# PSUM banks, one staged load, the weight splits and GpSimd's side jobs moved in the attention loops of an AdaLN block with experts

## The reference, cut to what matters

```
x: [4, 512, 256]                      # four batches of 512 tokens
mod = silu(c) @ wmod                  # per batch: shift, scale, gate of attention and of the FFN
h = layernorm(x) * (1 + ca) + sa
q, k, v = split(h @ Wqkv.T + bqkv)    # 16 heads of 16
scores = q k^T * 0.25, causal
attn = softmax(scores); x = x + ga * ((attn v) @ Wout.T + bout)
h = layernorm(x) * (1 + cb) + sb
top expert of 8 per token, its sigmoid scales the row
x = x + gb * (shared FFN(h) + FFN of the chosen expert)
```

## Time and profile before

| | |
|---|---|
| median of 3 runs | 470.62 us (469.96 to 471.55) |
| the profiled execution's own time | 467.88 us |
| its span, first to last instruction | 466.1 us |
| busy: PE, DVE, ACT, POOL | 86%, 67%, 49%, 45% |
| chain that ended last, by engine | PE 57%, DVE 16%, ACT 6%, POOL 6%, DMA 5% |
| mean granted TensorE clock | 0.969 |

### The profile page before, as it was taken

One profiled execution on the slowest core, in us unless ns is written; L12 is line 12 of the kernel. 1 busy time (PEld: TensorE's weight loads), 2 busy tenths in 40 slices (PEclk: granted clock), 3 DMA queues, 4 the chain that ended last, 5 costly groups with the idle time before them and its releaser, 6 DMA issues.

```text
span 466.1 us, 8603 instructions
## 1 busy us (share of the span) xinstructions
PE 401.6 (86%) x3009; PEld 226.4 (49%) x3009; DVE 313.4 (67%) x635; ACT 228.0 (49%) x408; POOL 211.4 (45%) x251
## 2 busy tenths in 40 slices
PE   3789984889879879878988878999998999999991
PEld 3244532334544446433544345565655666666660
DVE  7678594359888878998887853789844444444441
ACT  2445663577574757736777545345222323232320
POOL 2395952543227934368252862110510646464332
PEclk9999998699999999997999979999999999999997
DMA  8456489268942588945446201995531454434210
GB/s 269 159 131 143 164 237 227 91 184 212 257 112 90 175 190 261 288 133 169 128 137 213 62 1 46 344 358 202 148 123 46 73 96 72 89 65 87 27 20 0
DMA packets 46192, 67.96 MB, mean 146 GB/s; under 512 B 5380, under 2 KB 33668, under 8 KB 46152
## 3 DMA queue, kind: packets, MB, share of 16 engines
q1 hardware_dynamic: 31064, 36.74, 27.8%
q10 hardware_dynamic: 9936, 22.55, 14.8%
q0 software_dynamic: 5152, 8.14, 8.9%
HBM read 43.14 MB, written 25.18 MB: 147 GB/s over the span
## 4 chain that ended last, share of the span: by engine, by line
PE 57%; DVE 16%; ACT 6%; POOL 6%; DMA 5%; issue 5%; SPq 3%; ACTq 1%; DVEq 0%; POOLq 0%
PE bank L1504 35%; PE bank L1660 5%; PE bank L1644 4%; DVE mx L1137 3%; PE bank L1615 3%; DMA stage<-in_down 2%; PE bank L1885 2%; DMA qk_d<-W 2%; ACT W L887 2%; PE bank L1592 1%; SPq L532 1%; DVE x_sb L1182 1%; DVE rowg L1238 1%; POOL W L740 1%; POOL W L759 1%
## 5 line engine op out<-in xcount | busy, mean ns | idle before, releaser
L887 ACT ACTIVATE W<-bank 128x512 f32<-128x512 f32 (+1 forms) x176 | 93.8, 562 | 63.5 <-PE bank L1644 42.4
L1137 DVE TENSOR_REDUCE mx<-bank 128x1 f32<-128x384 f32 (+3 forms) x176 | 105.2, 633 | 26.2 <-PE bank L1617 22.5
L1504 PE MATMUL bank<-W 128*128 128x256 f16 (+2 forms) x756 | 104.7, 291 | 4.5 <-DVE x_sb L1182 1.8
L1504 PEld LDWEIGHTS bank<-W 128*128 128x128 f16 x756 | 73.0, 99 | 37.8 <-issue 8.2
L759 POOL TENSOR_SCALAR_AFFINE_SELECT W<-W 128x512 f32<-128x512 f32 x64 | 48.7, 764 | 86.9 <-ACT W L887 86.8
L1644 PE MATMUL bank<-W 128*128 128x512 f16 (+3 forms) x256 | 64.1, 308 | 20.1 <-ACT W L887 18.8
L1504 PE MATMUL bank<-W,h2T 128*128 x276 | 67.3, 380 | 0.8 <-issue 0.8
L830 POOL DMA_INDIRECT out<-h2T,sidx x23 | 36.3, 1578 | 64.1 <-DVE h2T L1474 63.8
L1615 PE MATMUL bank<-W 126*128 126x128 f16 (+3 forms) x208 | 53.6, 309 | 5.2 <-DVE mx L1137 4.7
L1660 PE MATMUL bank<-W 128*32 128x128 f32 (+3 forms) x512 | 49.6, 462 | 4.5 <-POOL W L759 4.4
L1644 PEld LDWEIGHTS bank<-W 128*128 128x128 f16 x256 | 21.5, 98 | 58.5 <-ACT W L887 36.7
(11 more groups left out here) (173 smaller groups left out, 557.3 us busy)
## 6 DMA issues: line engine op xcount, KB each, us to landing
w_d<-rowg ACTq DMA_DIRECT2D x18, 512.0 KB, 3.8
W<-w_d SPq DMA_DIRECT2D x18, 512.0 KB, 8.0
stage<-in_gup ACTq DMA_DIRECT2D x14, 512.0 KB
qk_d<-W SPq DMA_DIRECT2D x48, 128.0 KB
W<-qk_d SPq DMA_DIRECT2D x32, 192.0 KB, 5.5
stage<-in_down ACTq DMA_DIRECT2D x7, 512.0 KB
x_sb<-in_x SPq DMA_DIRECT2D x4, 512.0 KB, 8.9
h_d<-gbb SPq DMA_DIRECT2D x4, 512.0 KB, 4.6
```

The costliest lines, as they stand in the source:

```text
L887: a.activation(PT[j][:, i:i + m, :], t_bank(N)[:, 0:m * w].rearrange("p (i n) -> p i n", i=m), ACT.Exp).then_inc(s_exp, 1)
L1137: v.tensor_reduce(mx_v[:, b % 2, hp0 // 4, par, i:i + m, t], s_bank(N)[:, 0:m * w].rearrange("p (i n) -> p i n", i=m), AX.X, ALU.max).then ...
L1504: i = t_.matmul(outp, l, r, start=(n == 0), stop=(n == len(prods) - 1), **kw)
```

## The change

- The first pass goes round two banks (S0, S1) in the loops, the transposed pass round three (T0, T1, T2) all the way. The transposed unit 2 waits for the maximum of first-pass unit 32, which had T2 last. The waits follow the banks.
- SP issues the third staged load right behind `stacks(1, 0)`, ahead of `qk_out(1, 1)`, `stacks(1, 1)` and `mod_rows(0)`.
- SPLITS: eight weight units in b = 0 (n = 6, 12, 18, 23, 28, 33, 38, 43) where there were six, six in b = 1 at other steps, six in b = 2 (3, 10, 17, 24, 31, 38) where there were eight.
- POOL does its side jobs two steps later in the loops, save `rstd` and `bias_x`.

```diff
@@ SPLITS @@
-          0: {6: 0, 12: 1, 18: 2, 25: 3, 32: 4, 39: 5},
-          1: {2: 6, 9: 7, 16: 8, 23: 9, 30: 10, 37: 11},
-          2: {1: 12, 6: 13, 11: 14, 16: 15, 21: 16, 26: 17, 31: 18, 36: 19},
+          0: {6: 0, 12: 1, 18: 2, 23: 3, 28: 4, 33: 5, 38: 6, 43: 7},
+          1: {5: 8, 12: 9, 19: 10, 26: 11, 33: 12, 40: 13},
+          2: {3: 14, 10: 15, 17: 16, 24: 17, 31: 18, 38: 19},
...
+def gpsimd_jobs(b, n):
+
+    if b < 0:
+        return side_jobs(b, n)
+    prompt = ("stats1", "stats2", "bias")
+    return ([j for j in side_jobs(b, n - 2) if j[0] not in prompt]
+            + [j for j in side_jobs(b, n) if j[0] in prompt])
...
-        SB = [S0, S1, T2]
+        SB = [S0, S1]
...
-            return [S0, S1, T2, T0, T1, OTb][N % 6] if N < LAG else SB[N % 3]
+            return [S0, S1, T2, T0, T1, OTb][N % 6] if N < LAG else SB[N % 2]
...
-            return [T0, T1][N % 2] if N < BU * B - LAG else [T0, T1, T2][N % 3]
+            return [T0, T1, T2][N % 3]
...
             stacks(1, 0)
+            stage_load(2)
             qk_out(1, 1)
             stacks(1, 1)
             sp.wait_ge(s_md, 16)
             mod_rows(0)
-            stage_load(2)
...
-                    for job, c, k in side_jobs(b, n):
+                    for job, c, k in gpsimd_jobs(b, n):
...
-                if t_bank(N) is T2:
-                    pe.wait_ge(s_mx, BU * B)
+                if N == 2:
+                    pe.wait_ge(s_mx, LAG)
```

## The result

The changed kernel takes **468.4 us** (median of 20 runs, 464.0 to 472.74) against 470.24 (20 runs beside them); the ratio is 0.9939, 95% interval 0.9914 to 0.9964. The ratio leaves out the slow runs, those over 1.5% above the fastest of their kernel, so it says 2.9 us where the medians of all runs differ by 1.8. Against the 9.4 us that were forecast, the sign is right, the size is a third at most, and the forecast's own range of 456 to 467 us is missed by 1.4; the wide one, 453.0 to 470.0, holds it. The profiled execution took 466.85 us, span 465.1, granted clock 0.980 (before 0.969).

The account below looks back on a forecast made before the run. PE and DVE take turns at bounding the loops, with a stall in b = 0. Gains of 2.3 + 1.5 + 3.6 + 2.0 + 0 = 9.4 us off 470.62 give 461.2 us; forecast range 456 to 467, wide range 453 to 470.

Parts of the forecast that it names:

- Banks, taken as 0: Loops: fewer waits of transposed units for exps and more of first-pass units for maxima were taken to cancel; 0 us.
- the bounds, 18.6 us lost and 21.1 won: Banks in the loops: most that first-pass waits for maxima could lose, and most that waits for exps could return.
- The rival in which the first pass becomes the bound: Loops: PE waits for maxima and DVE lacks units; 9.2 us slower, 479.8 us, if all 18.6 are lost; chance 0.10.
- point of decision, 9.4 us lost: Banks: with half of the 18.6 us uncovered the time is 470.6, no change; above it the kernel is slower.
- Staged load, 2.3 us: Middle of b = 0: load issued earlier, ACT's wait goes, unit 22 starts at 83.4 us after the maxima's round trip.
- The first rival: Stall in b = 0: the maxima's trip ends when it did, only splits and masks are won; 465.0 us, chance 0.16.
- the sign set for it: Mark in b = 0: unit 22 starting at 85 us or later would show that the stall only changed its name.
- the second rival: Stall in b = 0: maxima share DMA engines with ACT's transfers, taking the load's 2.3 us; 463.5 us, chance 0.04.
- Clock behind the stall, 1.5 us: b = 0 behind the stall: PE stands about half as long, so the lower clock level may not fall or last less.
- Splits 3.6 and POOL 2.0 us: Splits: DVE time and half the lower-clock work in b = 2; POOL: about half of PE's 4.4 us mask waits.
- The mark "b = 2 shorter by 3 us": Sign for the splits: b = 2 shorter by 3 us or more; if as long as before, they did not set it.
- The rest: "no part of it to be given back": Behind the loops: unchanged work starts when they end, so none of the forecast 9.4 us was expected to be lost there.

Follow-up runs that it names:

- e3: The moved weight splits alone, on the kernel before; 471.46 us, ratio 0.9976.
- e4: The changed kernel with the banks of before (three for the first pass, two for the transposed pass); 465.85 us, ratio 0.9895 against the kernel before.
- e10: e4 with the staged load placed behind the writes of batch 1's second half, ahead of stacks, modulation rows and maxima; 462.95 us, ratio 0.9797.
- e12: The changed kernel with the third staged load put back behind the modulation rows; 471.01 us, ratio 1.0 against the kernel before.
- e15: e10 with PE's first-pass unit behind the values of each step instead of ahead of them; 464.43 us, ratio 0.9871 against the kernel before.
- e17: e10 with the new banks and PE's first-pass unit last in each step, behind values and side jobs; 462.79 us, ratio 0.9846.
- e7: e4 with the maxima of batch 0's second half sent out and in right behind the moved staged load; 472.18 us, ratio 0.9988.

## Why the prediction was right and wrong

**Banks, taken as 0: the step that failed.** The prediction said that where DVE is behind (residual, statistics, first norm) it "sets the pace with two banks as with three, and PE's wait moves without growing". It grew: 22 us more of first-pass waits, and 3.3, 2.1, 7.7, 3.9 and 6.7 us of time in five pairs, never a gain in this order of PE. I had looked at PE's wait and DVE's pace only; PE works in order, so the projections and transposed units queued behind the waiting unit waited too, and DVE then lacked units (with the banks alone, e1, 26.2 us of waits for PE, before 22.5; of the changed kernel's 28.9 the stall makes 7.7). In the traces the loops of the five pairs are 3.4, 3.7, 2.8, 0.4 and 5.6 us longer with the new banks. Of the bounds, 18.6 us lost and 21.1 won, the runs came nowhere near either: less than half of the one, about 2 of the other. The rival in which the first pass becomes the bound had the mechanism; its point of decision, 9.4 us lost, was not reached, so the kernel is not slower.

**Staged load, 2.3 us.** Unit 22 started at 83.37 us, and 83.4 was forecast, but that was luck: the maxima went out at 73.9 (in the sum 72.5), took 7.4 us (7.5), and PE followed 2.1 us later (3.4), so two errors cancelled. Nor is it the load's doing. Over the kernels traced here the exp of unit 22 starts at 83.4 to 86.3 us with the load where it was (seven traces, mean 84.8) and at 84.0 to 86.4 with it where the change put it (four, mean 85.0). The delay of the writes that the term counted (3.2 us, measured 3.7) ate all of it; only behind the writes does the load win (80.4 to 82.7, six traces). What unit 22 had gained in the changed kernel was gone at the start of b = 1, where PE waits 2.16 us for the second trip: 114.98 us, before 114.95. The first rival, the stall that changes its name, is what happened, though the sign set for it, unit 22 at 85 us or later, did not show. Why the kernel with the moved load was still 2.9 us faster beside the new banks and 2.7 slower beside the old stays open.

The Trainium skill's rule of the second rival (DMA: Bandwidth & Descriptors, Queues, rings and completion order) would have the maxima share the engines with ACT's transfers. This trace cannot decide on that: while the maxima waited, ACT's queue (q10) had little left to move, 0.03 MB against 1.19 of their own. But the rival had a point that the prediction missed, since ACT's two transfers, 1.05 MB issued at 70.0 and 70.4 us, came first. From 72 to 74 us the traffic was:

```profile
q10 hardware_dynamic: 157, 0.57, 100.0%
q1 hardware_dynamic: 3, 0.00, 0.4%
```

SP's stacks, issued from 71.53 on, stood still meanwhile, and the maxima are queued behind them. So ACT's transfers held up what stands ahead of the maxima, by some 2 us as an estimate from these two, and did not take turns with the maxima themselves.

**Clock behind the stall, 1.5 us.** Not won: the level falls all the same, since PE stands as long as before. It lasts 10.2 us in both kernels (from 78.8 us before, from 77.5 now); PE works through less of it, 4.3 us instead of 5.9, but the new stretch of 3.4 us at 115.1 takes that back.

**Splits 3.6 and POOL 2.0 us.** Together 5.6 were forecast, 7.7 measured (6.1 to 9.3 by the interval). That the sum came near is partly luck: one by one the terms measured 1.1 and 1.3, and that the two parts hide behind each other was not in the prediction. Of the places it named, the 4.91 us wait in b = 2 and the lower clock around it are gone (granted 1.00 there, 0.94 before), and PE waits 0.8 us for masks instead of 4.4. The longest of those waits, 2.04 us in b = 3, was worth 3.7 us by itself, because the clock no longer falls with it. The mark "b = 2 shorter by 3 us" still failed: in e3, too, b = 2 takes 53.3 us, since steps 12 to 22 lose 2.5 of the 4.1 us that steps 24 to 26 win.

**The rest: "no part of it to be given back".** In the two traces 2.9 us were. PE pauses at 334.74 for 2.83 us, which the chain of waits calls issue; every trace of this study has this pause in the shared FFN but the one of the kernel before that the sum was made against.

Sum over the parts in one order: splits and POOL 7.7 won, banks 7.7 lost, load 2.9 won, 2.9 in all; in another order the load loses and the banks lose less. The total is measured, the shares are not unique.

## What to carry to other kernels

A wait that is moved to another instruction of an in-order engine must be priced by what is queued behind it there, not by the engine's own idle time; at the one place that was followed here, two buffers took no longer than three once nothing long stood behind the wait, but that two do for three in the whole kernel was not shown. A small transfer that ends a stall should be followed back through its own queue: here 16 KB took 1.4 us on an empty queue and 7.4 to 11.1 behind a megabyte, and the rows that were moved out of its way were themselves due two steps earlier. Two parts that each give nothing may sit on two waits of the same step: try them together before dropping either.

## What the runs showed of the hardware

- From unit 32 to 34 of b = 3 the lower clock level goes with a wait of PE for a mask. In the six kernels where PE waits 1.8 to 2.05 us there, the level lasts 6.8 us; in the fourteen where it waits 0.31 us or less, it lasts 3.4 us in nine and does not come in five. Between e4 and the changed kernel, which both wait 0.31 us, this costs 1.3 us.
- Behind the loops the level comes and goes between kernels though the steps are the same: it appears in e10 from 331 to 338 us (granted 0.66 from 330 to 340), right behind the pause of PE, and in e12 to e15, while e17 has none. Behind the last exp the same work takes 177 to 184 us.
- So single effects of 1 to 3 us were not to be had from one trace. The 20 runs of the changed kernel lie from 464.0 us at a mean clock of 0.983 to 472.74 at 0.969.
- A low half on DVE takes 1.20 to 1.23 us in these traces where POOL does nothing beside it; beside POOL most take as long, but some up to 1.78. POOL can be slow then too: at 166.34 in e3 (above), beside a low half of 1.60 us, two masks take 2.21 us; at 93.75 in e7, with DVE idle, 1.21.
